# Queueing the steps that end a query block later in a fused attention and feed-forward kernel

## The reference

```
x = x + attn(layernorm(x))          # x: 16 x 2048 x 1024
x = x + ffn(layernorm(x))
# attn: qkv = x @ w_qkv + b; 16 heads of 64;
#       softmax(q k^T / 8) v; then @ w_proj + b_proj
# ffn:  h = x @ w1 + b1, rounded to multiples of 1/256;
#       piecewise-linear GELU between 33 points; @ w2 + b2
```

## Time and profile before

| | us |
|---|---|
| median of 3 executions | 2382.05 (2381.73 to 2637.96) |
| profiled execution, device time | 2378.78 |
| its span, slowest core (7) | 2377.2 |
| spans of the other cores | 2358.3 (core 1) to 2373.1 (core 2) |
| busy: PE, ACT, DVE, POOL | 2137.2, 1553.7, 1318.1, 224.4 |

### The profile page before, as it was taken

The page is one execution under the profiler, slowest core; times in us unless marked ns, Lnnn a source line. Parts: engine busy times, 40 slices in busy tenths (PEclk is TensorE's granted clock), DMA queues, the critical chain, the costliest instruction groups (busy, mean ns, idle before and its releaser), DMA issues.

```text
span 2377.2 us, 41375 instructions; the slowest of 8 cores (2358.3 to 2377.2 us)
## 1 busy us (share of the span) xinstructions
PE 2137.2 (90%) x14992; PEld 867.1 (36%) x14992; DVE 1318.1 (55%) x2134; ACT 1553.7 (65%) x1607; POOL 224.4 (9%) x321
## 2 busy tenths in 40 slices
PE   4888998987798998999998789999999999999997
PEld 2333333332233333333333234444444444444443
DVE  4244555533232433333345367888888887888772
ACT  4588898888688988888887634444444445445440
POOL 0100111112000110100002311000000000000001
PEclk8999999999899999999999989999999999999999
DMA  7444555556222332322125667544444444433322
GB/s 178 58 96 101 111 103 114 96 79 116 38 53 49 78 75 45 76 66 62 55 86 196 215 212 242 165 152 140 154 136 156 134 151 132 132 128 120 112 76 80
DMA packets 220294, 271.47 MB, mean 114 GB/s; under 512 B 138304, under 2 KB 142400, under 8 KB 219584
## 3 DMA queue, kind: packets, MB, share of 16 engines
q0 software_dynamic: 97968, 120.66, 22.5%
q1 hardware_dynamic: 122128, 148.16, 20.7%
HBM read 244.93 MB, written 71.57 MB: 133 GB/s over the span
## 4 chain that ended last, share of the span: by engine, by line
PE 35%; DVE 20%; DMA 15%; issue 14%; ACT 12%; SPq 3%; DVEq 0%; ACTq 0%; POOL 0%; POOLq 0%
ACT PT L715 8%; DMA rb<-denb 8%; PE pF L433 6%; PE pS L974 6%; PE pS L707 5%; PE pO L1030 5%; DVE nf L1007 4%; DVE g L1006 4%; DVE g L1005 4%; PE pF L497 3%; ACT g L998 3%; PE pO L730 3%; SPq L756 2%; PE pF L1030 2%; DMA denb<-dn 2%
## 5 line engine op out<-in xcount | busy, mean ns | idle before, releaser
L715 ACT ACTIVATE PT<-pS,gb 128x1024 bf16<-128x1024 f32 x1024 | 1064.5, 1112 | 199.5 <-PE pS L710 193.3
L974 PE MATMUL pS<-xn,w1s 128*128 128x512 bf16 x2048 | 776.9, 381 | 19.3 <-ACT n L981 16.5
L1030 PE MATMUL pO<-w2b,gbuf 128*128 128x512 bf16 x1792 | 658.7, 379 | 0.0
L707 PE MATMUL pS<-qp,kp 64*128 64x512 bf16 x1024 | 361.7, 386 | 95.9 <-ACT PT L715 91.5
L996 ACT ACTIVATE g<-nf 128x1024 f32<-128x1024 int16 x128 | 135.4, 1058 | 465.4 <-DVE nf L989 465.2
L710 PE MATMUL pS<-qp,kp 64*128 64x512 bf16 x1024 | 367.7, 391 | 0.0
L974 PEld LDWEIGHTS pS<-xn,w1s 128*128 128x128 bf16 x2048 | 200.6, 98 | 282.4 <-issue 58.9
L730 PE MATMUL pO<-PT,vt 128*32 128x512 bf16 x4096 | 275.0, 389 | 3.7 <-DVE de L753 2.5
L433 PE MATMUL pF<-xn,wqk 128*128 128x512 bf16 x1024 | 251.9, 383 | 3.1 <-DVE vt L505 2.1
L1030 PEld LDWEIGHTS pO<-w2b,gbuf 128*128 128x128 bf16 x1792 | 175.0, 98 | 201.6
L707 PEld LDWEIGHTS pS<-qp,kp 64*128 64x128 bf16 x1024 | 87.6, 93 | 400.3 <-issue 396.2
(11 more groups left out here) (111 smaller groups left out, 1649.7 us busy)
## 6 DMA issues: line engine op xcount, KB each, us to landing
w1s<-w1d SPq DMA_DIRECT2D x256, 256.0 KB, 3.2
xin<-x1s POOLq DMA_DIRECT2D x64, 512.0 KB, 6.5
rb<-denb SPq DMA_DIRECT2D x128, 128.0 KB
out<-xin POOLq DMA_DIRECT2D x28, 512.0 KB, 4.1
xin<-x SPq DMA_DIRECT2D x26, 512.0 KB, 9.4
x1s<-xin SPq DMA_DIRECT2D x26, 512.0 KB, 5.9
xffn<-x1s POOLq DMA_DIRECT2D x20, 512.0 KB, 5.5
wqk<-wqkv POOLq DMA_DIRECT2D x32, 256.0 KB, 7.2
```

The source lines that it names most:

```text
L707: pe.do(need, lambda e, kt=kt, sl=sl: e.matmul(pS[:, sl, 0:512], kp[0:64, r, kt * 128:(kt + 1) * 128], qp[0:64, r, qb * QB:(qb + 1) * QB], ...
L715: t = sc.do([t, gb_tok[g], pfree[pl_]], lambda e, sl=sl, pl_=pl_: e.activation(PT[:, pl_, :], pS[:, sl, :], AF.Exp, bias=gb[:, g:g + 1], s ...
L974: lambda e, dc=dc, h=h, wk=wk: e.matmul(pS[:, sl, h * 512:(h + 1) * 512], w1s[:, wk, dc, :], xn2[:, b % 2, dc, :], start=(dc == 0), stop=( ...
L1030: lambda e, hm=hm: e.matmul(obank[f], gbuf[b % 2][:, hm, tt * 128:(tt + 1) * 128], w2b[:, hm, cols], start=(hm == 0), stop=(hm == NHM - 1) ...
```

## The change

In each query block `step2` is queued 7 counts after the tail instead of 6, `step3` 12 instead of 8, and `step4` 19 instead of 14. Counted from the double step of the tail, as 0, they fall in double steps 8, 13 and 20 instead of 7, 9 and 15. A block has 8 double steps, so `step2` is now queued directly ahead of the next block's last `emit_pv` and tail, the product of a block comes half a block after the next block's tail, and `step3` comes one double step after the product of the block before. One `tick()` is added between the loop and its last `emit_pv`, and in the feed-forward part the ticks run for 7 steps `k` instead of 6, and `t_gbuf` and `load_b2` come at `k == 7`.

```
-            at(6, step2)
-            at(8, step3)
-            at(14, step4)
+            at(7, step2)
+            at(12, step3)
+            at(19, step4)
...
+        tick()
         emit_pv(*prev)
...
-            if k < 6:
+            if k < 7:
                 for _ in range(3):
                     tick()
-            if k == 6:
+            if k == 7:
                 t_gbuf.extend(att_store[(NG - 1, qb)] for qb in range(NQB))
                 load_b2()
```

## The result

The changed kernel takes 2347.7 us (median), against 2382.05 us before. The ratio is 0.9855, with a 95% interval of 0.9831 to 0.9878. A second measurement beside other kernels gave 0.9855 again (0.9832 to 0.9877). By the ratio that is 34.5 us less, where 47 were forecast. The profiled execution took 2346.08 us, its slowest core (4) spans 2344.5 us, the others 2332.9 to 2342.3.

What follows compares the result with a forecast made beforehand. PE and ACT were taken to bound attention in turn, stalled through DVE's order; 42 + 8.5 - 2.5 - 2 = 46 us off the profiled 2378.8 gave 2332.8, the median 3.3 above that, 2336, rounded to 2335. Range 2319 to 2360.

Steps and rivals of the forecast that it cites:

- The bound, and the wait that goes: Attention: PE and ACT bound in turn, stalled by DVE's product waiting for its broadcast; moving it later takes 42 us off.
- my sum: Whole kernel: 42 + 8.5 - 2.5 - 2 = 46 us off the profiled execution.
- step2, moved by one double step: Attention, DVE and SP: reciprocals right ahead of the copies, `dn<-de` beside `denb<-dn`; costs 2.5 us, bounds 0 to 6.
- slower: Rival, attention on SP: `denb<-dn` and `dn<-de` without their gap become the loop; 2400 us, chance 0.05.
- 42 - 2.5: Attention: 42 us of ACT's idle time behind late products goes, 2.5 us is lost to the later step2.
- 8.5 - 2: End of attention gains 6.2 us of PE's wait and 2.3 of clock; feed-forward loses 2, bounds 0 and 10.
- The crowd stays: Rival, attention: POOL's casting DMAs still delay landings, product or step2 stands at the three largest stalls; 2355 us, chance 0.17.
- SP comes free: Rival: waits for `pl` go too, 7 us plus clock, and ACT's small stalls shrink by 7; 2318 us, chance 0.16.
- Nothing: Rival, attention: ACT's stalls come from POOL's bursts and return as DVE waiting for `dn<-de`; 2380 us, chance 0.08.
- the forecast: Whole kernel: predicted 2335 us; its own case 2326 to 2344, a gain of 38 to 56, chance 0.54.
- The signs I had named: Attention and its end: broadcast wait under 20 us, guard never over 3, ACT's longest under 6, projection within 2, clock 1.00.

Runs made afterwards that it cites:

- s2_early: Changed kernel with step2 back at 6 (step3 12, step4 19 kept); 0.9805 and 0.9811 against the kernel before.
- mid: Kernel before with step3 at 9 and step4 at 16 in place of 8 and 14, step2 still at 6; ratio 0.9839.
- s2_only: Changed kernel with step3 and step4 back at 8 and 14, so only step2 is late; 1.007 against the kernel before.
- end_only: Changed kernel with the old places 6, 8, 14 for the first 61 query blocks, new ones for the last three; 0.9970 against the kernel before.
- paced_old: Kernel before, each of the 64 casting DMAs of w1 and w2 waiting for PE's last instruction before it; 0.9935, median 2364 us.

## Why the prediction was right or wrong

**The bound, and the wait that goes: right.** DVE's order and not its load held PE; the product behind the broadcast was the place. DVE's wait for it fell to 0.3 to 8.2 us by core, where I expected under 20. That the crowd would keep the product waiting did not happen. The part alone (s2_early) is worth 45 to 46 us, the 46 of my sum. The reciprocals' cost of 2.5 is absent there, so my sum without it was 48.5, 3 too high. How far the product has to go I did not see: I counted only the distance from broadcast to product, and mid has 38 us with the product moved by two double steps instead of five.

**step2, moved by one double step: this is the step that failed.** I priced it at 2.5 us, with bounds of 0 and 6, and it cost 10 to 12. The mechanism stood in the text: `denb<-dn` and `dn<-de` as neighbours on SP, and DVE waiting behind them in the crowd. Its size was wrong in three ways. I took the landings (up to 8.6 us) and the issue time of 5.67 us from stretches in which they happened to be shorter; in the changed kernel the four issues took 10.87 and the landing 12. I held that nobody is in a hurry for the sums, and did not follow the queue on: the store, the broadcast and the loads for the projection stand behind them, and SP waited 164 us there. And I costed the loads of `pl` at 0, bounds 7 on either side; they cost some 4 between the two profiled cores, and with two buffers most of the waits for them are gone. Of these, the stall in the crowd and `pl` are read from traces; that the 10 to 12 us are these two and nothing else is an argument. The rival "slower" had this mechanism, with its threshold and a chance of 0.05. It is at work in s2_only, which is slower by 0.7%, and at one block in the changed kernel. I had written that it would need a crowd at three or four places; s2_only shows that with the old place of the product small delays are enough, since each later broadcast makes a product wait that was waiting already.

**The sum by stretch.** PE's last work of attention ended at 1365.2 on the profiled core before and at 1336.5 on the one after, 28.7 us earlier, where I had 42 - 2.5 = 39.5. The stall in the crowd accounts for 11.17 - 0.42 - 2.5 = 8.3 of the difference. The two ACT stalls behind `pl`, 9.30 and 6.26 us after, 5.25 and 6.08 before, account for 4.2. Together they are 12.5, 1.7 more than the 10.8 that is missing, so the rest of attention gained a little more than I had. From there to the end of the span it is 1012.0 and 1008.0 us, 4.0 gained, where I had 8.5 - 2 = 6.5. I had the clock stay up after a pause of 1.5 us, and on the profiled core the pause was 2.78, for `pl`, and the clock fell. Whether 1.5 us would have kept it up the runs leave open: behind pauses of 1.3 to 1.7 us at this place it stayed at 1.00 on all eight cores of end_only and on six of mid, and fell to 0.50 for about three microseconds on the other two (1.38 and 1.66 us). What else was lost in the feed-forward part was not taken apart.

**The rivals.** "The crowd stays" gave 2355 and the range's upper part, and the measured 2347.7 lies between it and the forecast. It had the right stretch, and named the product or step2 at each of the three largest stalls: step2 stood, at one of them, and the product did not. "SP comes free" was wrong in sign, since the waits for `pl` grew; they went only with two buffers. "Nothing" is excluded by the result, by s2_early and by mid; what is right in it is that POOL's bursts carry a part, the 15 us of paced_old. The median lies within the range of 2319 to 2360 and within two per cent of the kernel before, but outside the forecast's own 2326 to 2344.

The fit by which the prediction estimated 2.3 us for a broadcast (the Trainium skill, "DMA: Bandwidth & Descriptors", section "Anatomy of one DMA") is one for DMAs issued from GpSimd, and the broadcast is issued on SP. The runs don't bear the estimate out either: the table has 9.8 us from the issue to the product that waited for it.

**The signs I had named.** Held: the product's wait, the guard, and roughly the last `ue`, 35 us earlier instead of 40. Failed: ACT's longest wait in attention (6.8 to 11.2 us, not under 6) and the start of the projection, 2.8 us after PE's last work, with half clock from 1340 us on. The sign that I had named for being wrong, a row of DVE's `dn` waiting for `dn<-de` with PE behind it, is there, and the waits for `pl`, which I had named beside it, grew.

## What to carry to other kernels

When steps of a chain are queued later, cost each one by itself: here one step's move gained 45 us and its neighbour's lost 11, and the sum hid both. A wait that moves between two DMAs of one queue is paid by everything behind them in that queue, so follow the queue on to the next load that somebody needs. If a buffer is all that ties two blocks together there, try a second one: here, with half a kilobyte on each of 16 partitions, it gave the changed kernel 18 us, more than moving step2 back did. Before moving a wait out of a crowd of DMAs, look whether the crowd itself is only a queue without pacing. And try the small move first: here two numbers changed, by one and by two double steps, gave 38 us.

## What the runs showed of the hardware that was not expected

The issue of a DMA on SP is itself slowed in a crowd. In the changed kernel four DMAs of 2 KB took 10.87 us to issue where 2.4 is usual, a store 2.91 where 0.37 is usual, and the two of the broadcast 2.86 where 1.14 is usual. The view of the DMA queues of that stretch, 559 to 571 us, shows the packets of the software queue at more than all 16 engines' time (so they must overlap in the counting) and the small DMAs landing after 12 us:

```profile
q0 software_dynamic: 5059, 1.30, 128.8%
...
dn<-de SPq DMA_DIRECT2D x4, 2.0 KB, 12.0
```

The crowd is one of small packets (5105 of 5112 under 512 bytes, 109 GB/s), so it is not seen in the bytes moved: from 1340 to 1343 us the same core moved 332 GB/s at a share of 1.08.

And an idle time of PE of 2.78 us was followed by three microseconds at half clock, 1.2 GHz, with PE busy all the time. Shorter pauses at the same place went either way: on mid's core 3 one of 1.34 us left the granted clock at 1.00, on its core 1 one of 1.38 was followed by some three microseconds at 0.50.
